# A four-layer gated transformer on one core: stage borders in another order, and gate rows spread by DMA

## What is computed

```python
x = x + tanh(g_xattn[L]) * attention_L(layernorm(x), ctx)
x = x + tanh(g_ffn[L])   * experts_L(layernorm(x))
```

```python
# layer 0: softmax over 40, top 6 of (scores + bias), 32 SiLU experts, 8 that pass x on
topk_w = take_along_axis(softmax(x @ Wc.T), topk_idx) * 2.5
# layer 1: softmax over 16, top 2 divided by their sum, shared SiLU expert with a sigmoid gate
rw, sel = top_k(softmax(x @ gate_w.T), 2);  rw = rw / rw.sum(-1)
# layer 2: softmax over 31 of (x @ Wr + br), top 3, GELU experts, shared expert, + x
# layer 3: softmax over 8, top 2, ReLU experts with 256 hidden features
out = out + w[:, e, None] * (act(x @ W1[e]) @ W2[e])
```

## Time and profile before

| | |
|---|---|
| runs | 736.62, 738.41, 739.43 us |
| the profiled execution | 738.34 us, its span 736.5 us |
| TensorE (PE) busy | 652.4 us, 89% |
| VectorE (DVE) | 531.7 us, 72% |
| ScalarE (ACT) | 378.5 us, 51% |
| GpSimd (POOL) | 270.8 us, 37% |
| granted TensorE clock, mean | 0.962 of full |
| experts of layers 0, 1, 2, 3 | 101.3 to 178.9, 296.4 to 348.1, 438.5 to 545.4, 678.0 to 731.5 us |

### The profile page before, as it was taken

One profiled execution on the slowest core, in us unless ns is written; L12 is line 12 of the kernel. 1 busy time (PEld: TensorE's weight loads), 2 busy tenths in 40 slices (PEclk: granted clock), 3 DMA queues, 4 the chain that ended last, 5 costly groups with the idle time before them and its releaser, 6 DMA issues.

```text
span 736.5 us, 11957 instructions
## 1 busy us (share of the span) xinstructions
PE 652.4 (89%) x3653; PEld 457.8 (62%) x3653; DVE 531.7 (72%) x1298; ACT 378.5 (51%) x652; POOL 270.8 (37%) x463
## 2 busy tenths in 40 slices
PE   2787679998899988998999899999988899979997
PEld 2575547775676655675566546777766676645764
DVE  5482788887877537987864569888877988544886
ACT  1544254543467632553466337777744565622774
POOL 7723356663210003363111216666742000020673
PEclk9997689999999998999999999999999999998999
DMA  8211042110000010010000301111100010100111
GB/s 284 92 73 72 0 157 73 43 44 0 2 4 31 18 59 0 23 44 11 1 4 21 99 0 38 36 43 43 37 7 1 4 32 3 32 0 1 37 43 36
DMA packets 24087, 28.50 MB, mean 39 GB/s; under 512 B 4002, under 2 KB 19938, under 8 KB 24036
## 3 DMA queue, kind: packets, MB, share of 16 engines
q1 hardware_dynamic: 24036, 27.87, 12.2%
HBM read 22.22 MB, written 5.24 MB: 37 GB/s over the span
## 4 chain that ended last, share of the span: by engine, by line
PE 68%; DVE 20%; ACT 4%; issue 4%; POOL 2%; DMA 1%; DVEq 0%; SPq 0%; ACTq 0%; POOLq 0%
PE PS L653 10%; PE PS L654 10%; PE PS L655 10%; PE PS L675 4%; PE PS L879 4%; PE PS L516 4%; PE PS L788 3%; PE PS L862 3%; DVE consts L1503 2%; DVE negmax L1497 2%; DVE qst L1457 1%; PE PS L894 1%; DVE hid_lo L1412 1%; PE PS L859 1%; DVE xn L1224 1%
## 5 line engine op out<-in xcount | busy, mean ns | idle before, releaser
L414 POOL TENSOR_TENSOR wpair<-ring,ones_col 128x128 fp32r<-128x128 f32 (+1 forms) x150 | 78.7, 525 | 139.2 <-PE PS L655 98.7
L1406 DVE TENSOR_TENSOR pT<-pT,PS 128x512 f32<-128x512 f32 x150 | 102.5, 684 | 28.7 <-ACT pT L1050 22.8
L1149 ACT ACTIVATE pT<-PS 128x512 f32<-128x512 f32 x160 | 92.1, 592 | 49.2 <-PE PS L862 39.7
L1412 DVE TENSOR_TENSOR hid_lo<-pT,hid_hi 128x512 fp32r<-128x512 f32 x150 | 112.0, 746 | 2.3 <-ACT hid_hi L1057 1.4
L416 POOL TENSOR_TENSOR wpair<-ring,wpair 128x128 fp32r<-128x128 f32 (+1 forms) x150 | 103.5, 690 | 11.7
L1057 ACT ACTIVATE hid_hi<-pT 128x512 fp32r<-128x512 f32 x150 | 93.8, 625 | 12.4 <-DVE pT L1406 12.1
L653 PE MATMUL PS<-hid_hi,wpair 128*128 128x512 f32 x150 | 86.6, 577 | 5.8 <-DVE hid_lo L1412 5.8
L653 PE MATMUL PS<-xhi,wpair 128*128 128x512 f32 x204 | 85.3, 418 | 2.5 <-DVE pT L1406 1.9
L1050 ACT ACTIVATE pT<-PS,ring 128x512 f32<-128x512 f32 x96 | 65.9, 689 | 36.6 <-PE PS L655 36.6
L654 PE MATMUL PS<-xlo,wpair 128*128 128x512 f32 x204 | 82.5, 404 | 0.0
L655 PE MATMUL PS<-xhi,wpair 128*128 128x512 f32 x204 | 82.4, 404 | 0.0
(11 more groups left out here) (239 smaller groups left out, 1289.6 us busy)
## 6 DMA issues: line engine op xcount, KB each, us to landing
ring<-in_mlp SPq DMA_DIRECT2D x48, 128.5 KB, 2.1
ring<-in_glu SPq DMA_DIRECT2D x27, 192.0 KB, 2.4
keys<-qst SPq DMA_DIRECT2D x18, 256.0 KB, 2.0
kz<-keys SPq DMA_DIRECT2D x36, 128.0 KB, 3.1
qst<-kfull SPq DMA_DIRECT2D x96, 4.0 KB
wq<-in_wq SPq DMA_DIRECT2D x3, 256.0 KB, 4.3
consts<-in_consts SPq DMA_DIRECT2D x1, 740.0 KB, 5.1
x_res<-in_x SPq DMA_DIRECT2D x1, 512.0 KB, 3.8
```

The source lines that it names most:

```text
L1149: act.activation(pT[:, w % 8, :], PS[:, 2 + w % 2, :], ACT.Exp, scale=sc).then_inc(A["p"], 1)
L1406: dve.tensor_tensor(hid[:, hf, :], src[:, hf, :], PS[:, 6 + hf, :], ALU.mult).then_inc(M["hid"], 1)
L1412: dve.tensor_tensor(hid_lo[:, kept, :], hid[:, kept % 2, :], hid_hi[:, kept, :].bitcast(f32), ALU.subtract).then_inc(M["lo"], 1)
```

## The change

Six things, all in one edit:

- **Gate rows by DMA.** The gates of half 1 are transposed as fp32 rows (four more transposes into bank 7), copied by ScalarE to `gate_rows`, saved to DRAM by SyncE, and from entry 2 on (`by_pe = 2`) SyncE sends each entry's row back to 64 + 64 partitions of one of four slots. VectorE reads that slot where it read PSUM. 67 of 150 spreads are gone.
- **Ring.** The first four slots are filled by `fill_ring` ahead of `attention(L)`; GpSimd splits entries 0 and 1 ahead of the norm's `rstd`. `load_ring` first waits for `rows_out`, saves the rows and waits for that, sends the gates of entries 2 and 3, and only then stacks keys and enters its loop.
- **Norm and logits.** Half 0 is turned, copied and multiplied with the router's weights before the attention ends; the logits lie in banks 6 and 7.
- **Routing of layers 1 to 3** ranks the logits. The softmax's sum is taken beside or behind, and divided at the end.
- **Fillers.** 30 matmuls on zeros become 13, 22 and 10; 16 become 8; 6 become 4; 4 new ones stand ahead of the last outputs. `start_results` goes behind `up(2)`.
- **Elsewhere.** `split_query_weights` waits for the last `lo`; `prepare_masks` goes in six steps into the end of layer 0's experts; some load semaphores are joined and `negk` takes other memory.

```diff
+        gate_rows = pT[0:EP, 7, :]
+        gate_slot = [consts[...], consts[...], consts[...], gate_own[:, :]]
+        by_pe = 2
...
+            def fill_ring(L, w, cols):
+                if L > 0:
+                    sp.wait_ge(mo[L - 1]["y"], UP_AHEAD + 2 * ROUTE[L - 1]["ENT"])
+                for k in range(RING):
+                    sp.dma_start(ring[:, k, 0:cols], w[k, :, :]).then_inc(ring_in[k], 16)
...
+                def spread_gate(e, k):
+                    for side in range(2):
+                        row = gd[L][bass.ds(2 * e + side, 1), :] if glu else gd[L][bass.ds(e, 1), :]
+                        sp.dma_start(gate_slot[k][side * 64:side * 64 + 64, :],
+                                     row.broadcast_to([64, HALF])).then_inc(gate_in[k], 16)
...
+                sp.wait_ge(rows_out, L + 1)
+                sp.dma_start(gd[L], gate_rows[:, :]).then_inc(rows_saved, 16)
+                sp.wait_ge(rows_saved, 16 * (L + 1))
+                for e in range(by_pe, RING):
+                    spread_gate(e, e)
...
                         sp.dma_start(ring[:, k, 0:cols], w[RING * i + RING + k, :, :]).then_inc(ring_in[k], 16)
+                        spread_gate(RING * i + RING + k, k)
...
+                    elif e == 0:
+                        layer_norm(2 * L + 1)
...
             def split_query_weights(L):
+                pool.wait_ge(mo[L - 1]["lo"], 2 * ROUTE[L - 1]["ENT"])
...
             def turn_weights(L):
+                for i in range(4):
+                    mm = pe.transpose(PS[0:EP, 7, i * P:(i + 1) * P], wtab[:, 4 + i, :], ident)
+                mm.then_inc(rt["tr"], 1)
...
-                    keep_busy(7, 30)
+                    keep_busy(0, (0, 13, 22, 10)[L])
...
+                spread(0, 0, 0)
+                pe.wait_ge(rows_out, L + 1)
+                spread(1, 0, 1)
...
-                            spread(u + 2, RING * i + k + 1, hf)
+                            if hf == 0:
+                                spread(u + 2, RING * i + k + 1, hf)
...
-                keep_busy(5, 6)
+                layer_norm(2 * L + 1, (0,))
+                keep_busy(5, 4)
                 turn_normalised(1)
                 keep_busy(5, 3)
                 project_outputs(1)
-                keep_busy(5, 16)
+                route(L, 0)
+                keep_busy(5, 8)
...
+                act.wait_ge(rt["tr"], 2 * L + 2)
+                act.activation(gate_rows, PS[0:EP, 7, :], ACT.Copy).then_inc(rows_out, 1)
...
-                link(dve.tensor_reduce(rmax[:, :], shifted[:, :, 0:SM], AX.X, ALU.max))
+                run(dve.max(top8[:, i, :], scores[:, i, 0:SM]) for i in range(NT))
+                if L > 0:
+                    dve.tensor_tensor(shifted[:, :, 0:SM], scores[:, :, 0:SM], top8[:, :, 0:1].broadcast_to([P, NT, SM]),
+                                      ALU.subtract).then_inc(rt["shift"], 1)
...
+                    else:
+                        gate = gate_slot[slot]
+                        dve.wait_ge(gate_in[slot], 32 * turn + 32 * (gates_before[L][slot] + (slot >= by_pe)))
+                    dve.tensor_tensor(hid[:, hf, :], src[:, hf, :], gate, ALU.mult).then_inc(M["hid"], 1)
```

More of the change, by code:

```diff
@@ L160, in build @@
         yT = oT
+        gate_rows = pT[0:EP, 7, :]
+        gate_own = sb("gate_own", [P, HALF])
+        gate_slot = [consts[:, C_DFT:C_DFT + HALF], consts[:, C_DFT + HALF:C_DFT + 2 * HALF], consts[:, C_BAND:C_BAND + HALF],
+                     gate_own[:, :]]
+        gd = [nc.dram_tensor(f"gates{L}", (EP, HALF), f32, kind="Internal").ap() for L in range(4)]
         pick64 = qf[0:PARTS * EP, :].bitcast(bf16)
@@ L212, in build @@
         k_saved = [sem(f"k_saved{n}") for n in range(4)]
-        kz_set, kz_in = sem("kz_set"), [sem(f"kz_in{b}") for b in range(B)]
+        kz_in = [sem(f"kz_in{b}") for b in range(B)]
         ac = {n: sem("ac_" + n) for n in ("kin", "kine", "kfreq", "kfe", "qin", "qine", "qfreq", "prod", "corr", "top",
@@ L231, in build @@
         mo = [{n: sem(f"mo{L}_{n}") for n in ("wstep", "wup", "wdown", "up", "spread", "act", "gated", "hid", "hi", "lo", "y",
-                                            "yT", "ytr")} for L in range(4)]
+                                            "yT", "ytr") if n != "gated" or L < 2} for L in range(4)]
+        rows_out, rows_saved = sem("rows_out"), sem("rows_saved")
+        gate_in = [sem(f"gate_in{k}") for k in range(RING)]
+        by_pe = 2
+        gates_before = [[sum(len([e for e in range(by_pe, ROUTE[M]["ENT"]) if e % RING == k]) for M in range(L))
+                         for k in range(RING)] for L in range(4)]
         x_done = sem("x_done")
@@ L978, in _ @@
             layer_norm(1)
-            route(0)
+            for hf in range(NHALF):
+                route(0, hf)
             experts(0, True)
@@ L982, in _ @@
                 attention(L)
-                layer_norm(2 * L + 1)
-                route(L)
+                layer_norm(2 * L + 1, (1,))
+                route(L, 1)
                 experts(L, L < 2)
@@ L1390, in add_input, with unit @@
                                                       in1=x[:, i, :], op0=ALU.mult, op1=ALU.add))
-                def unit(u, kept, hf_first=False, first=False):
+                def unit(u, kept, entry, slot, turn=0, hf_first=False, first=False):
                     hf = kept % 2
@@ L1404, in unit @@
                         dve.wait_ge(M["gated"], u + 1 + UP_AHEAD)
-                    dve.wait_ge(M["spread"], u + 1)
-                    dve.tensor_tensor(hid[:, hf, :], src[:, hf, :], PS[:, 6 + hf, :], ALU.mult).then_inc(M["hid"], 1)
+                    gate = PS[:, 6 + hf, :]
+                    if slot is None:
+                        dve.wait_ge(M["spread"], u + 1)
+                    elif hf == 0:
+                        dve.wait_ge(M["spread"], entry + by_pe + 1)
+                    else:
+                        gate = gate_slot[slot]
+                        dve.wait_ge(gate_in[slot], 32 * turn + 32 * (gates_before[L][slot] + (slot >= by_pe)))
+                    dve.tensor_tensor(hid[:, hf, :], src[:, hf, :], gate, ALU.mult).then_inc(M["hid"], 1)
                     if not glu and not first:
@@ L1415, in experts @@
                 for u in range(2 * RING):
-                    unit(u, u % KEPT, hf_first=(u < 2), first=(u == 0))
+                    unit(u, u % KEPT, u // 2, None if u // 2 < by_pe else u // 2 % RING, hf_first=(u < 2), first=(u == 0))
                     add_input(u)
```

180 lines of the change are left out of this document (101 added, 79 removed).

## The result

The changed kernel took 744.76 us (median; 742.77 to 746.44) against 738.11 for the kernel before (736.62 to 739.43). The ratio is 1.009 with a 95% interval of 1.0055 to 1.0124: slower, by little, and certainly not the 721 of the forecast. The profiled execution is the fastest of these, 742.77 us with a span of 741.0; against the span before, 736.5, that is +4.5.

What follows compares the result with a forecast made beforehand. TensorE was taken to bound the experts' loops, VectorE the borders and SyncE the first entries. From 738.34 us, -13.6 - 15.8 - 1.9 + 1.7 + 7.1 + 5 = -17.5 gave 721, range 709 to 731.

Steps and rivals of the forecast that it cites:

- A, the loops: Experts' loops: 67 spreads removed, 59 of them gaining 0.230 us each on TensorE; -13.6 us.
- inside the room of 0.56 - 0.23 = 0.33: Experts' loops: VectorE's product over SBUF adds 0.03 us an entry, which its remaining idle time of 0.33 covers.
- Rival three: Loops of layers 2 and 3: VectorE becomes the bound, moved products take 1.21; +7.6 us, 729; chance 0.12.
- most meet none: Loop before: most VectorE operations with two SBUF inputs meet no GpSimd operation that blocks them; mean 722 ns.
- B, the borders: Borders before the experts: earlier routes, shorter chains, fewer fillers; layers 1 to 3 gain 7.7, 2.4 and 5.7; -15.8 us.
- C, the ends: Ends of loops: the query split moved behind the last lo no longer runs beside VectorE's L1412; -1.9 us.
- D, the starts: First entries: four transposes and ScalarE's row copy ahead of the second spread, mask steps in layer 0's tail; +1.7 us.
- E, entry 4: Layers 0 and 2: entry 4's weights load only after row save, gate DMAs and key stacks; +2.6 and +4.5, sum +7.1 us.
- F, the clock: TensorE's granted clock falls to 0.50 after idle stretches at the stalls of layers 0 and 2 and the borders; +5 us.
- rival five: Layers 2 and 3: SyncE becomes the bound through two gate DMAs an entry; at 1.6 us each, 755; chance 0.04.

Runs made afterwards that it cites:

- e10: The changed kernel with the old fillers: 30 ahead of the weight transposes in layers 1 to 3, 16 ahead of half 1's turning; 745.9 us, ratio 1.0096.
- e11: The changed kernel with GpSimd's split of the query weights no longer waiting for the last rest (hid_lo); 747.72 us, ratio 1.0139.
- e4: The changed kernel with GpSimd splitting only 8 of 128 weight columns from entry 4 on in layers 2 and 3, work left out; 730.13 us.
- e6: The changed kernel without gate rows by DMA: TensorE spreads all entries, key stacks wait for the attention alone; 726.61 us, ratio 0.9865.
- e2: The changed kernel with SyncE's key stacks and layer 0's mask loads back ahead of the wait for the gate rows; 737.51 us.
- e12: Changed kernel plus four hid buffers, key stacks first, 8 fillers behind last transposes, layer 0 gates by TensorE, 16 fillers ahead of half 1's turning; 718.92 us.
- e7: The kernel before with four buffers for the gated hidden rows (hid) instead of two; 741.3 us, ratio 1.0066.

## Why the prediction was wrong

It forecast -17.5 against the profiled execution; the trace of after has +4.5 in the span. A slower kernel had a chance of 0.04, all of it for SyncE as the bound of layers 2 and 3; the bound was VectorE. The terms:

- **A, the loops: -13.6 forecast, about -1.6 measured.** This is the step that failed. The price of a spread was right: layer 1 runs at 4.35 instead of 4.60 an entry, layer 0 at 4.34 in its middle, the first entries of layer 3 at 2.98. Wrong was "inside the room of 0.56 - 0.23 = 0.33". I read the 15.0 us of idle time in the earlier trace rows as room. Of the 0.28 a unit, 0.19 is the hand-over from the rest directly ahead, which lay hidden under ScalarE's name because ScalarE came later still. The room was 1.61 - (0.60 + 0.722 + 0.19) = 0.10 a unit, 0.2 an entry, less than the 0.23 to be taken. At full pace nothing was left for a rest longer than 0.70, and it became 0.88. That growth is the larger part: with the rest at 0.722 the same sum gives 2 x 1.512 = 3.02 an entry, with 0.877 it gives 3.34. The prediction priced only the moved product and took the old rest as unchanged, without a reason.
- **Rival three** had the right engine with a chance of 0.12 and the wrong piece of it. It let the moved product grow by 0.52; the product stayed at 0.73 in layer 2 and the old rest grew. The reading that in the loop before "most meet none" was wrong as well: there too a row of GpSimd lies beside each rest, and the rests alternate between 0.68 and 0.78 (486.30 and 487.91 above). Where the product did grow, to a mean of 976 ns in the `consts` slots of layer 0, it cost nothing, since the longer entries of two `up` pairs have room.
- **B, the borders: -15.8 forecast, -12.2 measured**, by border -5.7 (7.7), -1.3 (2.4), -5.2 (5.7). The route was right to 0.1 in layers 1 and 2 (1.65, 1.31). Too large was the gain ahead of the route: 2.6 instead of 4.3 in layer 1, and in layer 2 a loss of 0.7 instead of a gain of 0.8. Part of both is the low clock: where it is full there, row to route take 10.7 in layer 1 and 10.65 in layer 2 (e10), gains of 3.3 and 0.4. In layer 2 the sum also took the whole 0.73 behind the parts, which its text calls mostly a hand-over that stays; 0.06 of it is left, so the sum was right there and the text was not.
- **C, the ends: -1.9 forecast.** The wait is worth about 3 (e11). But the stretch behind layer 0 is 2.0 longer, from the low clock at its end. Without a low clock there, it has +0.1 in e4 and, with no gate rows besides, -1.0 in e6.
- **D, the starts: +1.7 forecast, about +3.9 measured.** Layer 1 +0.9 as forecast; layer 3 +2.2, of which 1.6 is a low stretch of this execution (e2 has +0.6); the mask steps 0.8 instead of 0.3, because VectorE had no room there.
- **E, entry 4: +7.1 forecast, +10.0 measured**, with layer 0 +4.4 and layer 2 +5.6. The mechanism, the order of SyncE and the load 14.0 behind the transpose were right, and e2 shows them. In layer 2 the landing was taken at 2.1 and GpSimd waited 4.0. Too small was layer 0: from the stacks' end to the load were 3.1 us instead of 2.1, so that the load stood at 116.8 instead of 115.6, and `up` came 5.6 behind it instead of 5.0.
- **F, the clock: +5 forecast.** Behind the two stalls 2.2 more were lost in one entry, behind layer 0 2.0, in layer 3 1.6: some 6 in places that can be named, of which the last two are counted in C and D already; what it cost at the borders is inside B. By the mean granted clock, 0.962 and 0.949, the low level lasted 736.5 x 0.038 / 0.5 = 56 us before and 76 after. The size was about right. Half of it was forecast for layer 2's stall, where 0.9 fell; that the sum of the places came near 5 is in part luck.

The bounds I gave to A were only those of a longer product. Had I written VectorE's unit as a sum of distances between starts, as I did for TensorE, the loop would have come out at 3.02 an entry with the rest of the earlier trace rows, with VectorE as the bound and every further 0.1 us of the rest costing 0.2 an entry. That would have shown the danger, not its size: what the rest would grow to, no row of the kernel before tells.

## What to carry to other kernels

Idle time before an instruction is not room. Its releaser is only the last of several waits, and one that is nearly as late stands right behind it: add up the engine's own cycle from start to start, with every wait on itself, and compare that with the new period before another engine's work is removed. A buffer count of two that makes an instruction wait for the one directly ahead of it is such a cycle; two more buffers were worth 10.9 us here, and in the kernel before, whose bound lay elsewhere, they gained nothing (it was 0.7% slower). And an instruction that the change does not touch can still change its length: `hid_lo` did, and that was the larger part of the loss. And a transfer that must wait for a late result belongs behind the ones that need not, on the same queue: that order alone was worth 7.3 us.

## What the runs showed of the hardware

- An instruction of VectorE that waits for the one directly ahead of it starts 0.19 us after its end in most cases (0.09 to 0.20 in layer 2's loop); one that does not starts 0.08 before its end (480.37 against 479.50 + 0.95). The Trainium skill, "VectorE: DVE Perf Modes", section "The DRAIN you can't avoid", says of eight copies in a row that a semaphore behind each costs nothing extra. For a signal alone no run here says otherwise; a wait for it on the same engine cost 0.27 here, ahead of a product over PSUM.
- A gate row to 64 partitions costs SyncE 0.56 to 0.62 of issue (1.24 / 2 at 438.90), no more than a key stack (7.66 / 12 = 0.64), and lands after 2.9 to 3.0. Of the feared bound by SyncE (rival five) nothing was seen. The page's rows on DMA issues:

```profile
consts<-gates SPq DMA_DIRECT2D x98, 128.0 KB, 2.9
...
gate_own<-gates SPq DMA_DIRECT2D x36, 128.0 KB, 3.0
```

- The rest over two SBUF operands took 685 ns with GpSimd's instructions at 0.20 to 0.28 us, 722 in layer 2's loop when TensorE bounded it, and 877 when VectorE did, with the same number of GpSimd instructions an entry. Why it is longer in the last case was not found.
- A low clock between the attention's last row and the route of layer 2 goes with a longer stretch: 10.65 and 10.66 us in the two traces at the full clock (e10, e12), 11.72 in the changed kernel's with 4.0 us of it. Of the variants of the changed kernel, those with 8 fillers at this place have it and the two with 16 do not; but e7, with 16, has 2.4 us of it and 11.88.
